# Mamba and routed attention, fused: another order of TensorE's steps around the block boundaries of the Mamba half

## What is computed

```python
u = _layernorm(x, ln_w, ln_b)
zxbcdt = u @ in_proj_w.T
z   = zxbcdt[..., :D_INNER]                                   # 1024
xBC = zxbcdt[..., D_INNER:D_INNER + CONV_DIM]                 # 1024 + 2 * 128
dt  = jax.nn.softplus(zxbcdt[..., -NHEADS:] + dt_bias)        # 16 heads
xBC = jax.nn.silu(causal_depthwise_conv(xBC, 4 taps) + conv_b)
xs, Bm, Cm = split(xBC)
A = -jnp.exp(A_log); dA = jnp.exp(dt * A)
def step(state, inp):
    state = state * dA_t[:, :, None, None] + (dt_t[:, :, None] * x_t)[..., None] * B_t[:, None, None, :]
    y = jnp.einsum('bhpn,bn->bhp', state, C_t)
y = (scan(step) + D * xs) * jax.nn.silu(z)
y = y * jax.lax.rsqrt(jnp.mean(y * y, -1, keepdims=True) + EPS) * gamma
return x + y @ out_proj_w.T
```

## Time and profile before

| what | value |
|---|---|
| median of 3 runs | 4204.06 us (4194.79 to 4207.88) |
| the profiled execution, its own time | 4202.89 us |
| its span, first to last instruction | 4200.5 us |
| mean granted clock of TensorE | 0.945 |
| busy share of TensorE, VectorE, ScalarE, GpSimd | 88%, 73%, 61%, 44% |
| HBM traffic | 66 GB/s |

### The profile page before, as it was taken

One profiled execution on the slowest core, in us unless ns is written; L12 is line 12 of the kernel. 1 busy time (PEld: TensorE's weight loads), 2 busy tenths in 40 slices (PEclk: granted clock), 3 DMA queues, 4 the chain that ended last, 5 costly groups with the idle time before them and its releaser, 6 DMA issues.

```text
span 4200.5 us, 72564 instructions
## 1 busy us (share of the span) xinstructions
PE 3691.8 (88%) x28414; PEld 2188.1 (52%) x28414; DVE 3078.1 (73%) x5404; ACT 2567.7 (61%) x4781; POOL 1828.9 (44%) x1513
## 2 busy tenths in 40 slices
PE   4789999999999999999824979998999989999998
PEld 2455555555555555555412545555566546655555
DVE  4778887877888877887565766677777767777773
ACT  4666766666766666765421565666666666666665
POOL 0233333332333332332221777765555555555555
PEclk7899999999999999999966999999999999999998
DMA  4223323233222232222213343434333343333332
GB/s 124 58 69 73 76 41 79 69 71 77 70 48 71 69 79 71 69 59 50 41 48 54 74 92 70 77 73 91 78 76 73 73 93 76 73 73 71 67 67 39
DMA packets 297669, 294.28 MB, mean 70 GB/s; under 512 B 38663, under 2 KB 223623, under 8 KB 295280
## 3 DMA queue, kind: packets, MB, share of 16 engines
q1 hardware_dynamic: 241008, 186.70, 17.4%
q0 software_dynamic: 56320, 102.94, 14.1%
HBM read 176.19 MB, written 101.71 MB: 66 GB/s over the span
## 4 chain that ended last, share of the span: by engine, by line
PE 66%; DVE 15%; DMA 6%; ACT 5%; issue 4%; POOL 3%; SPq 1%; POOLq 0%; DVEq 0%; ACTq 0%
PE pair L1020 9%; PE pair L1103 8%; PE pair L1066 8%; PE pair L1266 6%; PE pair L1113 5%; PE pair L1183 3%; DMA rbc<-rank 3%; PE pair L1085 3%; PE pair L1158 3%; PE pair L1094 3%; PE pair L1171 2%; PE pair L1045 2%; PE pair L1199 2%; DVE state L1468 2%; PE pair L1145 2%
## 5 line engine op out<-in xcount | busy, mean ns | idle before, releaser
L1411 DVE SCALAR_TENSOR_TENSOR cv<-raw,taps,cv 128x512 f32<-128x512 f32 x480 | 462.8, 966 | 36.5 <-ACT cv L1808 32.2
L1650 DVE TENSOR_REDUCE smx<-pair 128x2 f32<-128x514 f32 x512 | 346.6, 684 | 137.5 <-PE pair L1199 137.4
L2077 POOL TENSOR_TENSOR ph<-pf,ph 128x512 f16<-128x512 f32 x256 | 323.7, 1268 | 198.5 <-ACT ph L1941 197.3
L1020 PE MATMUL pair<-xhT,whi 128*128 128x512 f16 x1280 | 383.2, 381 | 0.0
L2082 POOL TENSOR_TENSOR ohl<-of,ohl 128x256 f16<-128x256 f32 x256 | 209.8, 820 | 307.1 <-ACT ohl L1946 307.0
L1266 PE MATMUL pair<-whi,oT 128*128 128x512 f16 x1024 | 329.1, 383 | 1.1 <-ACT xq L1902 1.1
L1066 PE MATMUL pair<-whi,xhT 128*128 128x512 f16 x1024 | 327.1, 381 | 2.5 <-ACT raw L1794 2.5
L1589 DVE TENSOR_SCALAR_CACHE_REDUCE rjunk<-rbc,cst 128x640 f16<-128x640 f16 (+1 forms) x192 | 185.5, 966 | 182.6 <-DMA rbc<-rank 180.3
L1103 PE MATMUL pair<-ohi,yT 128*128 128x512 f16 x1024 | 316.8, 381 | 1.1 <-ACT yT L1865 1.1
L1158 PE MATMUL pair<-xq,whi 128*128 128x512 f16 x1024 | 310.9, 386 | 0.7 <-ACT xk L1902 0.7
L1838 ACT ACTIVATE de<-de,cum 128x128 f32<-128x128 f32 x1024 | 310.7, 390 | 0.7
(11 more groups left out here) (245 smaller groups left out, 10623.8 us busy)
## 6 DMA issues: line engine op xcount, KB each, us to landing
de<-cum SPq DMA_DIRECT2D x64, 1024.0 KB, 9.5
rows<-rowt SPq DMA_DIRECT2D x16, 1040.0 KB, 4.2
xin<-x SPq DMA_DIRECT2D x16, 1024.0 KB, 5.3
y<-xin SPq DMA_DIRECT2D x16, 1024.0 KB, 10.4
y<-ob POOLq DMA_DIRECT2D x64, 256.0 KB, 4.0
rbc<-rank SPq DMA_DIRECT2D x64, 256.0 KB, 3.4
qb<-qa SPq DMA_DIRECT2D x32, 512.0 KB
wst<-wkv SPq DMA_DIRECT2D x32, 256.0 KB, 3.1
```

Of the source, the lines that this page charges most:

```text
L1020: ins = pe.matmul(bk[:], w[:, k, ws], xt[:, ha, k, :], start=n == 0, stop=n == 3 * KD - 1)
L1411: ve.scalar_tensor_tensor(c_[:], r_[:, t:t + BLK], taps[:, ct, t:t + 1], c_[:], ALU.mult, ALU.add).then_inc(done, 1)
L1650: ve.tensor_reduce(smx[:, qt, 2 * h2:2 * h2 + 2], sc[:, :, 0:NK + 1], AX.X, ALU.max)
L2077: po.tensor_tensor(p_[:, 1, 1], f[:, 1], p_[:, 0, 1], ALU.subtract).then_inc(S.plp, 1)
```

## The change

It changes four things. The convolutions of the next block are woven in from -0.15 to 1.1 in place of -0.25 to 1.05. A `Part` at share 1 no longer empties its feed but drives it to its `end`. The `turns` feed is driven from -1.4 to 0.5 in the block in which it starts, and from 0.5 to 2.6 in the next (before: to 0.35, and from 0.35). And `conv` waits for the four `turn_out` of its block.

```diff
-CONV_START, CONV_END = -0.25, 1.05
+CONV_START, CONV_END = -0.15, 1.1
...
     def to(self, share):
-        self.feed.to(1 if share >= 1 else self.start + share * (self.end - self.start))
+        self.feed.to(self.start + share * (self.end - self.start))
...
     for i in range(NBLK):
         others = []
         if i + 1 < NBLK:
-            others.append(Part(ahead, 0.35 if i else 0, 2.6))
+            others.append(Part(ahead, 0.5 if i else 0, 2.6))
             others.append(Part(Feed(convolutions(i + 1), NCT * 2.6, record), CONV_START, CONV_END))
         if i + 2 < NBLK:
             ahead = Feed(turns(i + 2), TURNS, record)
-            others.append(Part(ahead, -1.4, 0.35))
+            others.append(Part(ahead, -1.4, 0.5))
         weave(Feed(back(i), CK * 21.6, record), *others)
...
             def conv(i, ct):
+                q.wait_ge(S.xT, CK * (i + 1))
                 wait_given_back(q, "conv", i, ct)
```

## The result

The changed kernel takes **4079.98 us** in the median of four runs (4075.65 to 4085.52), the kernel before 4204.65. The ratio of the means is 0.9708, with a 95% interval from 0.9686 to 0.973: 2.9% faster. The forecast was 4074. The profiled execution has a span of 4082.2 us, 118.3 less than before. The edit added a line, so that L1030 of before is L1031 now, and every later line is one further.

What follows compares the result with a forecast made beforehand. TensorE was taken as the bound, waiting out the dt chain before `cum`. Saving 9.0 us in 14 blocks plus 3.0 and 1.3 at the ends gives 130, so 4074 us; range 4045 to 4105, high end 4140 with VectorE's case.

Steps and rivals of the forecast that it cites:

- The half clock: At block boundaries, TensorE's clock halves around the wait for `cum`; saves 1.67 on slow `cum`, about 1.3 on other work.
- The dense block: Four dense chunks less two convolutions, plus turns, `logits` and `cum` at full clock: 114.7 us before the new waits.
- the signs named: No wait at `cum`, no half clock between 290 and 2000 us, `cum` groups of 2.0 us, period near 116.
- `logits`: New TensorE wait between `gate` and `logits`: 1.75 us delay, 1.34 covered by turn and gate, 0.41 left.
- `open` behind the silu: New wait at the next block's `open` for the tenth convolution's silu: 14.68 us against 13.8 of TensorE work, 0.85.
- The DVE margin: Change in TensorE's small waits on VectorE per block: bounds -1.7 and +2.5 us, taken as 0.
- the paragraph on the queues: No instruction or DMA added or removed, apart from one wait; `cum_store` moves with `cum`, on POOL only places shift.
- The sum: A new block of 116.0 us saves 9.0, times 14 is 126; with the ends 130 us in all.
- The terms of the ends: One-time gains: 3.0 us at block 15's `open`, 1.3 us in block 0 at `gate`.
- VectorE as the bound: Rival, chance 0.13: contention with GpSimd adds up to 33.8 us a block; at half paid, block 118.7, time 4112.
- `open` waiting long for the tenth silu: Rival, chance 0.04: silu ends 24.4 us after its convolution's start, `open` waits 10.6, block 127.2, time 4231 us.
- The wait that only moves: Rival, chance 0.05: VectorE runs the dt chain just ahead of `cum`, the 6.4 us return one chunk on; 4200.

Runs made afterwards that it cites:

- e3: Changed kernel with a Part at share 1 emptying its feed again, so `cum` stands right behind `logits`: 4173.68 us, ratio 0.9924 to the kernel before.
- e2: Kernel before with only the convolutions moved to their new places; turns, `logits` and `cum` at their old ones: 4204.74 us, ratio 1.0002.
- e1: Changed kernel with the convolutions back at their old places, turns and `cum` at the new ones: 4102.13 us, ratio 0.9759 to the kernel before.
- e5: Changed kernel with the first statistics of a later block's x planned later on VectorE, behind `y_in` of the second chunk: 4041.38 us, ratio 0.9618.
- e8: e5 with `dxs` computed twice in every chunk, to load VectorE with 4.9 us a block more: ratio 0.9641, period 114.06.
- e9: e5 with `dxs` computed four times in every chunk, 14.7 us a block more on VectorE: ratio 0.9926, period 121.33.
- e12: Changed kernel with the pause behind `logits` cut from 12 to 3, leaving 8.2 us of TensorE work ahead of `cum`: ratio 0.966, period 115.59.
- e7: e3 with its wait in front of `cum` filled by 28 matmuls whose results are thrown away (the filler): ratio 0.9817, period 120.82.

## Why the prediction was right

*The bound.* TensorE was it, and the wait in front of `cum` was the price: putting back the one line that moves `cum` gives 2.2 of the 2.9% back (e3), and the convolutions' move alone gives nothing (e2). Beside the rest it is worth 22 us, all at the two ends (e1).

*The half clock.* Its share was taken as 1.67 + 1.3 = 3.0 us a block; the filler measures 2.69.

*The dense block.* I had 114.7 us with its waits of 0.42. The block of e5, which has no other waits, is 114.05: right within 0.7. Of the signs named, `cum` waits for nothing, its groups take 2.0 us and the period is under 119. One sign failed: there are stretches of clock 0.50 between 290 and 2000 us, three of 3.4 us in the steady blocks and three in block 15.

*The new waits.* `logits`: 0.41 taken, 0 measured. `open` behind the silu: 0.85 taken, 0.98 to 1.3 measured, 11.4 us in 11 blocks; the race came out nearly as worked out, 13.9 us of TensorE's work against a silu that ends 14.8 us behind its convolution's start. The DVE margin: 0 taken. It is the term that was too small: `open` waits behind `state_out` 27.9 us in 35 pieces between 523 and 1850 us, where 0.42 each would be 14.7, so 13.2 us in 11.3 blocks, 1.2 a block; `conv` behind z_silu adds 0.2, and three of the waits at `open` were followed by 3.4 us at half clock, 0.4 a block. With the 114.05 and the silu's 1.0 that makes 116.8 of the 117.2. The rows of one chunk, on which I rested the zero, showed that VectorE can be 92% busy without holding TensorE. They couldn't show in which order it would work. Nor did the paragraph on the queues take up the load of x, which the new order made late.

*The sum.* A block saves 7.7 in place of 9.0. The terms of the ends were too small in turn: block 0 gained 12.8 for 10.3 taken, block 14 3.5 for 3.0, block 15 5.8 and the start 1.6 for nothing. So 124.2 of 130 us came in the Mamba half, and that the sum came so near is in part luck: blocks 0 to 13 gained 113.3 us where 127 were taken, and what blocks 14 and 15 and the start gained beyond the 3.0 taken, 7.9, covers more than half of the gap. Block 0 is luck inside: the 5.24 us in front of `open` of block 1 weren't foreseen, and were outweighed by the end of the waits in front of `gate` (4.43) and `cum` (7.8) and by 13 us less at half clock. The attention half took 5.8 us more with the same instructions; it varied from 2062.7 to 2073.5 over the profiles of that chip, and I leave it there.

*The rivals.* VectorE as the bound: no, at the load of the forecast, though in the order of e5 (e8); at 9 us more it costs 7.3 us a block (e9). The high end of the range has a slip: 60% of the 33.8 us paid gives some 4159 us, and 4140 stands for 56%. The contention of the taps with GpSimd is there: they need 0.752 us in the median and up to 2.391. "GPSIMD Engine Reference", section Specifications, of the Trainium skill says that VectorE shares its SBUF interfaces with GpSimd and that instructions with two SBUF inputs contend, and the trace agrees. But packing didn't raise it in the changed kernel. The group of taps in one block of the changed kernel, the counterpart of the earlier trace rows, and then the taps of e12, 500 to 1800 us:

```profile
L1412 DVE SCALAR_TENSOR_TENSOR cv<-raw,taps,cv 128x512 f32<-128x512 f32 x30 | 25.9, 871 | 3.3 <-ACT cv L1809 3.2
...
L1412 DVE SCALAR_TENSOR_TENSOR cv<-raw,taps,cv 128x512 f32<-128x512 f32 x331 | 334.6, 1024 | 44.9 <-ACT cv L1809 43.7
```

A tap takes 871 ns on average in the changed kernel's block, 982 before. In e12 it takes 1024, VectorE is busy 101.2 us a block, about as before, and the block is the shorter one, 115.59. How often the two engines meet thus goes with the order rather than with the packing; no run tries it by itself. `open` waiting long for the tenth silu: no, 1.3 us at most in the steady blocks. The wait that only moves: no, and at 8.2 us of cover it doesn't either (e12).

## What to carry to other kernels

A step whose input is a chain of small dependent instructions should not stand right behind the step that starts the chain. Other work of the engine that bounds hides it, and here 8.2 us of it hid a chain that had been waited for 6.4 us, with 0.5 us to spare; the 20 us of the change hid no more. The chain itself got longer, 7.5 us, once the other engines had work beside it, so some margin is needed. Count such a wait at more than its length where it also lowers the matmul clock. Once the large wait is gone, the order on the second-busiest engine can matter more than its load: here an order was worth 3 us a block and 5 us more of load cost nothing. The order was found by planning one step later; swapping the same step by hand lost 2.5 us a block.

## What the runs showed of the hardware

Behind the wait in front of `cum`, 6.2 to 7.8 us, the granted clock of TensorE was half in every boundary of the kernel before, for 10.2 or 13.7 us beginning 0.6 to 3.3 us into the wait; with the same time filled with matmuls that nobody reads, the granted clock stays 1.00 and the kernel is 1.1% faster than e3 (e7). Short waits do it at times: in the changed kernel those of 2.16, 3.19 and 1.33 us in front of `open` were followed by 3.4 us at half clock, one of 2.86 us was not. The window behind the first, in the changed kernel:

```profile
646.30:649.60 3.30, 3.30 (x11) 2.52 (x12) 3.23 (x7) 2.14 (x5) 2.66 (x2) 0.50 0.00 0
```

VectorE's busy time for the same instructions isn't a constant: 101.8 us a block before, 97.1 in the changed kernel, 96.7 in e5 and 101.2 in e12, with GpSimd at 40.7 to 41.7. And the changed kernel's two profiles, on different occasions, differ by 31 us in the attention half (2068.5 and 2099.7) and by nothing in the Mamba half; no run here says why.
